# One number in an attention kernel's order: the transposition of the coming quad's maxima stands behind two pieces instead of four

## The reference

```
xn = layernorm(x)                                   # x: (4, 1024, 256)
S = einsum('hid,hjd->hij', K, Q) * SCALE
S = where(delta < 0, -inf, S) + (-delta)            # delta = i - j
C = softmax(S, axis=-1);  attn = einsum('hij,hjd->hid', C, V)
s = attn @ o_w.T + o_b
g = silu(moe(xn))                                   # top 2 of 8 experts, exact gelu
out = x + s * g
```

## Time and profile before

| | |
|---|---|
| runs | 709.43, 714.72, 719.42 us; median 714.72 |
| profiled execution | 710.94 us, span of its instructions 709.1 us |
| granted clock of the tensor engine | 0.989 of full speed over the span |
| busy share of the span | PE 96%, PEld 65%, DVE 76%, ACT 68%, POOL 33% |
| a window (first half-score to the next window's) | about 25 us, 16 of them, from 113 to about 520 us |

### The profile page before, as it was taken

How to read it: one execution, slowest core, us unless ns; L and a number is a source line. 1 busy time by engine, 2 the same in 40 slices (tenths; PEclk the granted TensorE clock), 3 DMA queues, 4 the chain that set the end, 5 groups by cost and what they waited for, 6 DMA issues and landing times.

```text
span 709.1 us, 17536 instructions
## 1 busy us (share of the span) xinstructions
PE 681.8 (96%) x6039; PEld 461.3 (65%) x6042; DVE 536.7 (76%) x1146; ACT 484.6 (68%) x994; POOL 236.1 (33%) x336
## 2 busy tenths in 40 slices
PE   6998999999999999999999999999999999999885
PEld 3885676455555556555555655554479899999764
DVE  6566988899989988898998998997234654444298
ACT  4552345577877777778787777778876666666374
POOL 5331211242023424333342332200035847575300
PEclk9999999999999999999999999999999999999998
DMA  6999895063485576477568558710279686955396
GB/s 210 313 246 372 294 286 183 9 103 83 78 167 136 139 172 156 132 142 171 130 137 173 135 140 149 158 55 19 62 185 295 215 218 206 238 179 173 117 400 247
DMA packets 74903, 124.46 MB, mean 176 GB/s; under 512 B 14184, under 2 KB 44392, under 8 KB 74696
## 3 DMA queue, kind: packets, MB, share of 16 engines
q1 hardware_dynamic: 65200, 95.17, 52.9%
q0 software_dynamic: 9616, 28.17, 12.7%
HBM read 72.56 MB, written 49.72 MB: 172 GB/s over the span
## 4 chain that ended last, share of the span: by engine, by line
PE 76%; DVE 11%; DMA 7%; ACT 3%; issue 2%; SPq 1%; POOL 0%; DVEq 0%; POOLq 0%; ACTq 0%
PE ps L1600 18%; PE ps L1531 13%; PE ps L1584 12%; PE ps L1689 8%; PE ps L1711 8%; PE ps L1520 6%; PE ps L1480 4%; DVE mxa L1122 4%; DMA q_parts<-arena 2%; PE ps L1490 2%; PE ps L1672 2%; ACT arena L983 2%; DVE x_room L1435 1%; DVE arena L1430 1%; DVE arena L1420 1%
## 5 line engine op out<-in xcount | busy, mean ns | idle before, releaser
L1122 DVE TENSOR_REDUCE mxa<-ps 128x1 f32<-128x512 f32 (+3 forms) x608 | 358.5, 656 | 35.0 <-PE ps L1520 18.9
L983 ACT ACTIVATE arena<-ps 128x512 f32<-128x512 f32 x576 | 303.4, 605 | 80.5 <-PE ps L1584 41.2
L1531 PE MATMUL ps<-aug 57*128 57x512 f32 (+3 forms) x768 | 219.4, 401 | 3.2 <-DVE mxa L1122 1.1
L1584 PE MATMUL ps<-aug 59*128 59x512 f32 (+3 forms) x768 | 216.3, 398 | 0.9 <-ACT arena L983 0.5
L1584 PEld LDWEIGHTS ps<-aug 59*128 59x128 f32 x768 | 110.4, 185 | 77.1 <-ACT arena L983 69.6
L1600 PE MATMUL ps<-arena,v_q 128*32 128x512 f32 (+3 forms) x1536 | 154.5, 497 | 0.9 <-ACT arena L983 0.9
L1531 PEld LDWEIGHTS ps<-aug 57*128 57x128 f32 x768 | 109.9, 185 | 39.8 <-DVE mxa L1122 25.1
L876 POOL DMA_INDIRECT xs_dram<-arena,slot x64 | 62.6, 978 | 76.3 <-ACT arena L983 72.5
L903 POOL DMA_INDIRECT y_dram<-arena,y_row_of x71 | 69.4, 978 | 47.9 <-DVE y_row_of L1359 39.5
L1520 PE MATMUL ps<-key_mask,key_rows 64*128 64x64 bf16 (+2 forms) x704 | 79.1, 208 | 0.0
L1520 PE MATMUL ps<-query_mask,query_rows 64*128 64x128 bf16 (+1 forms) x640 | 75.4, 211 | 0.0
(11 more groups left out here) (149 smaller groups left out, 641.3 us busy)
## 6 DMA issues: line engine op xcount, KB each, us to landing
aug<-k_parts SPq DMA_DIRECT2D x96, 128.0 KB
aug<-q_parts SPq DMA_DIRECT2D x96, 128.0 KB
arena<-xs_dram SPq DMA_DIRECT2D x71, 128.5 KB, 2.6
k_parts<-arena SPq DMA_DIRECT2D x16, 512.0 KB, 6.2
q_parts<-arena SPq DMA_DIRECT2D x16, 512.0 KB, 5.9
arena<-y_dram SPq DMA_DIRECT2D x16, 512.0 KB, 6.8
xn_dram<-arena SPq DMA_DIRECT2D x8, 512.0 KB, 7.3
a_dram<-arena SPq DMA_DIRECT2D x128, 32.0 KB
```

What stands on the lines that cost most here:

```text
L983: nc.scalar.activation(prob_slot(q, i), score_bank(q, i), ACT.Exp).then_inc(exp_done, 1)
L1122: nc.vector.tensor_reduce(dst, src, AX.X, ALU.max).then_inc(piece_used, 1)
L1531: ins = nc.tensor.matmul(banks[:, at_ * width:(at_ + 1) * width], k_aug[n][rows, hp, ib * P:(ib + 1) * P], q_aug[n][rows, hp, lo:lo + widt ...
L1584: ins = nc.tensor.matmul(out_[:, col0:col0 + hi - lo], q_aug[n][rows, h // SIDES_OF_ARRAY, jb * P:(jb + 1) * P], k_aug[n][rows, h // SIDES ...
```

## The change

`AHEAD_OF_MAXIMA` is the number of pieces of quad q+2 ahead of the transposition for quad q+1. It goes from 4 to 2. `stream` is used by PE and DVE alike, so both orders move.

```diff
@@ -113,7 +113,7 @@
 COUNTS_AT = 20
 ROUTE_FROM = 3
 AHEAD = 14
-AHEAD_OF_MAXIMA = 4
+AHEAD_OF_MAXIMA = 2
 PACE = 2
 STORE_BESIDE = 8
 NLOAD = 2 * SIDES_OF_ARRAY * len(K_PART)
```

## The result

| | before | changed |
|---|---|---|
| median of 9 runs, us | 712.23 (708.54 to 719.42) | 723.64 (721.73 to 726.09) |
| ratio, 95% interval | | 1.0158 [1.0129, 1.0186] |
| profiled execution: time, span | 710.94, 709.1 | 724.14, 722.2 |

The change costs 11 us, 1.6%: a clear loss, though less than 2%. The forecast was 721.0 (711 to 729) and slower by 8.3.

The account below looks back on a forecast made before the run. It took three engines handing work to each other, over a chain almost wholly of tensor work, as the bound. 14 x 0.70 = 9.8 us of cost less 1.5 of gain, +8.3 on 712.8, gave 721 us, range 711 to 729.

Parts of the forecast that it names:

- step 1: Tensor engine at the transposition: it waits for the split of the maxima, 0.38 us a window.
- Step 2: Tensor queue from transposition to half-score 25: the new order pairs pieces and half-scores worse, 0.33 us a window.
- the rule: Tensor array at the transposition: one more layout entry a window, some 0.11 us, hidden behind the wait; otherwise 1.5 us more.
- Step 3: Scalar run of 8 exponentials after batch 4: it passes the delay to batch 5, making the window about 0.7 us longer.
- the absorbed case: Tensor engine after batch 4: the wait is absorbed and only the gain of 1.5 us is left, 711.3 us; chance 0.2.
- Step 4: Vector engine at pieces 3 and 4: 0.24 us lost, piece 4's reduction 0.34 late, covered by the scalar run.
- The fixed distance of batch 5 to the split: Each window: batch 5 follows the split by a fixed time, so 0.7 us holds for late splits too.
- The worse case: After batch 4 the vector engine sets the pace and its 0.34 us adds: +13.2 us, 726.0; chance 0.15.
- Step 5: Window starts: maxima's row transfers go 1.1 us earlier, regaining late starts of 1.5 us in sum.
- The sum: Whole kernel: cost of 9.8 us over 14 windows less the gain of 1.5, +8.3 us.
- The base of 712.8: Starting time for all cases, the middle between the profiled execution and the median of three runs before.

Follow-up runs that it names:

- short_split_two: The changed kernel with two of the three split operations left out after quad 0, so it doesn't compute the whole; 720.20 us, 1.0106 against the kernel before.
- moved_alone: Against the kernel before: transposition behind two pieces, pieces 2 and 3 still beside half-scores 23 and 24 ahead of batch 4; ratio 1.0196, in a second set 1.0106.
- ahead_of_batch: Against the kernel before: transposition still behind four pieces, but just ahead of batch 4 instead of behind it; ratio 1.0114.
- two_transfers: The kernel before, old order, with the parts of the maxima carried by two transfers of two rows instead of four of one row; ratio 0.9988.
- five_pieces: Against the kernel before: transposition behind five pieces instead of four; ratio 0.9956 on the slow chip, 1.0044 when run again.
- one_piece: Against the kernel before: transposition behind one piece instead of four; 734.16 us, ratio 1.0299.
- batch_first: Against the kernel before: batch 4 right behind half-score 22, then the transposition, pieces 2 and 3 kept beside half-scores 23 and 24; ratio 1.0194.

## Why the prediction was right

**The direction and its cause**: step 1 said that the transposition would wait for the split in 13 or 14 windows where it had waited in one. It waits in 14.

**Step 1, the wait.** 0.38 a window was forecast, 0.25 measured. PE doesn't come to the transposition where it came to piece 2, as I had it, but 0.13 later, as entering the full array takes that long. The hop of 0.03 to 0.04 that I took for one between engines was read between two operations of DVE; from DVE to PE it is 0.05 (245.56 to 245.61).

**Step 2, the order.** 0.33 was forecast, 0.57 measured (short_split_two). The 0.13 ahead of the transposition is in it, 0.08 is the lonely piece 3, which takes 0.42 up to half-score 25 and not 0.34, and the remaining 0.03 is the hop and rounding of rows. This is the term that was too small. The sum of steps 1 and 2 was 0.71 and is 0.82, as the entry was counted in neither and took from the wait what it added to the order. The Trainium skill, TensorEngine Tiling (Array Packing), Key Properties, says that a change of tiling mode drains TensorE. The trace agrees in kind: 0.47 against 0.34 in short_split_two, where the split was done 0.23 sooner. In the changed kernel the wait covers it, as I had supposed, so the rule changed the split between the two steps and not the time.

**Step 3, whether it reaches the end.** It does, in full. ACT's run is again 4.03 us without a gap, and batch 5 moved by 0.80 as half-score 25 did. This is what the absorbed case denied, and it is out.

**Step 4, DVE.** A pause of 0.24 was expected ahead of piece 3, 0.39 came, and it is covered. The fixed distance of batch 5 to the split, 5.39 before, is 6.19 to 6.20 in 13 of the windows and 6.31 in window 0. The worse case, in which DVE's lag is added, is out: it needs windows 1.05 longer and they are 0.82 longer. The lag itself is 0.50 and not 0.34 (the reduction of piece 4 starts 3.35 after the split, before 2.85). Added to the 5.36 at which batch 5 came when DVE did set it (window 11 before), it gives 5.86, and batch 5 comes at 6.19.

**Step 5, the gain.** 1.5 us were forecast. The five late starts before made 1.85 us together (windows 1, 6, 7, 8 and 12 started 8.46, 8.48, 9.28, 8.46 and 8.32 after their splits, and the usual is 8.23); in the changed kernel all are at 9.04 to 9.16. So all of it came back, and was lost six times over.

**The sum.** 14 x 0.82 - 1.85 = 9.6 against 10.1 between the windows of the two traces. The rest is 0.8 more of late splits, less 0.4 because window 0 grew by only 0.42. 8.3 was forecast and 11.4 measured between the medians. The part that is not in the windows, 1.3 us, is open; the runs of one kernel differ by more. The base of 712.8 that I took was near the median of 712.23.

**What was not foreseen** is a second path to the same DVE. The ring of four banks binds the item four places behind piece 0 to the end of its reduction, 0.7 us after the split. The old order has the transposition there, behind a batch. moved_alone puts piece 3 there and ahead_of_batch the same transposition, without the batch between. Their windows are 0.64 and 0.38 longer, with the wait for the split included in the first.

No version that computes the whole beats the kernel before on the faster chips: two_transfers (0.9988) can't be told from it. five_pieces was faster on the slow chip alone.

## What to carry to other kernels

Moving an operation up for the sake of its result moves everything behind it on the same queue back: price first how long its input has been ready at the old place (1.45 us here) against how far it moves (1.66 us, from 239.72 to 241.38: half-score 22 is loaded at 239.25 and the entry takes 0.47), and then what the neighbours lose in pairing. A gain from earlier data is bounded by the late starts that it can remove (1.85 us in 16 windows), and these can be read before anything is changed. Where several engines hand work round in a window, count the distances from the one event that the moved step hangs on; lengths of windows tell differences of 0.1 us, which whole runs with 1% of spread don't.

## What was not expected of the hardware

A transposition between two half-scores that use 64 rows costs 0.13 us ahead of it besides its own 0.23 (0.47 against 0.34 from load to load).

The granted clock of PE stayed at its upper level through nearly all windows, though PE waited in each. It fell in two windows of one_piece, where PE waited longest, and in the three of batch_first named above. Stretches of one_piece from window start to window start:

```profile
204.30:230.50 26.20, 25.57 (x281) 14.60 (x277) 23.05 (x43) 19.89 (x38) 7.63 (x10) 1.00 0.69 139
230.50:261.70 31.20, 30.17 (x283) 16.61 (x279) 24.56 (x43) 20.52 (x38) 9.00 (x13) 0.84 0.56 120
...
445.70:473.80 28.10, 27.28 (x281) 15.43 (x277) 23.48 (x43) 19.89 (x38) 7.67 (x10) 0.94 0.66 136
```

The window with a mean of 0.84 took 31.2 us instead of 26.2, and that with 0.94 took 28.1, together 6.9 us more. That execution took 736.67 us. The one with the highest mean clock, 0.993, took 728.18, which is 17.4 above the kernel before, and the others at 0.977 and 0.980 took 734.83 and 733.48. So a part of the 21 us between the medians goes with the clock, beside the 17 of its windows at full clock. Whether the waits brought the clock down, one execution can't show.

One of the chips ran the kernel before in 729.69 us (17 runs, 725.76 to 733.43), the others in 710.8 to 712.6 (medians). The order of two versions was not the same on it (five_pieces: 0.9956 there, 1.0044 elsewhere).
